# A graph network on one core: layer 3's state and the neighbour sums turned by block transpose and device memory

## The reference, cut to what matters

```python
def first(x, adj, weight, bias):                       # x 16x512x128, adj 16x512x512
    adj_norm = adj / (adj.sum(-1, keepdims=True) + 1e-8)
    h_neigh = einsum('bnm,bmf->bnf', adj_norm, x)
    return relu(concatenate([x, h_neigh], -1) @ weight + bias)

def gated(x, adj, mask, weight, w_ih, w_hh, b_ih, b_hh):
    A = (adj != 0)
    h = x
    for l in range(5):
        m = einsum('bnd,de->bne', h, weight[l])
        agg = einsum('bij,bid->bjd', A, m)
        h = gru_cell(agg, h, w_ih, w_hh, b_ih, b_hh)   # r, z, n gates; (1-z)*n + z*h
    return h * mask[..., None]

x = layernorm(x + first(x, adj, ...))
x = layernorm(x + gated(x, adj, ...))
```

## Time and profile before

| | |
|---|---|
| median of 3 runs | 609.21 us (609.12 to 609.42) |
| the profiled execution | 608.95 us, span 606.9 us |
| PE busy | 589.7 us, 97% of the span |
| DVE busy | 513.5 us, 85% |
| ACT busy | 419.4 us, 69% |
| POOL busy | 419.4 us, 69% |
| chain that ended last | PE 91%, DVE 4%, all else 1% or less each |
| granted TensorE clock | 0.992 of full over the span |

### The profile page before, as it was taken

How to read it: one execution, slowest core, us unless ns; L and a number is a source line. 1 busy time by engine, 2 the same in 40 slices (tenths; PEclk the granted TensorE clock), 3 DMA queues, 4 the chain that set the end, 5 groups by cost and what they waited for, 6 DMA issues and landing times.

```text
span 606.9 us, 9921 instructions
## 1 busy us (share of the span) xinstructions
PE 589.7 (97%) x2733; PEld 479.4 (79%) x2733; DVE 513.5 (85%) x1151; ACT 419.4 (69%) x777; POOL 419.4 (69%) x335
## 2 busy tenths in 40 slices
PE   7999999999999999999999999999999999999992
PEld 6678788888888888888888888888888888877771
DVE  5986969898998989899898989989898898966677
ACT  5767685958778595876868587685867768555451
POOL 0645464878868687886869688687977868755343
PEclk9999999999999999999999999999999999999996
DMA  8713122454344446334444534445453433010101
GB/s 271 294 35 114 54 76 88 134 180 121 123 151 112 161 127 190 121 121 146 115 154 138 190 112 130 141 115 158 138 174 110 148 138 95 10 53 10 44 0 53
DMA packets 74002, 73.55 MB, mean 121 GB/s; under 512 B 5760, under 2 KB 49280, under 8 KB 73984
## 3 DMA queue, kind: packets, MB, share of 16 engines
q1 hardware_dynamic: 73712, 73.20, 37.7%
q10 hardware_dynamic: 272, 0.13, 0.1%
HBM read 56.00 MB, written 17.30 MB: 121 GB/s over the span
## 4 chain that ended last, share of the span: by engine, by line
PE 91%; DVE 4%; DMA 1%; issue 1%; ACT 1%; SPq 1%; POOL 0%; POOLq 0%; DVEq 0%
PE ps_tok L1405 12%; PE ps_tok L1412 12%; PE ps_r L1269 6%; PE ps_r L1270 6%; PE ps_r L1271 6%; PE ps_z L1269 6%; PE ps_z L1271 6%; PE ps_z L1270 6%; PE ps_b L1271 3%; PE ps_b L1269 3%; PE ps_b L1270 3%; PE ps_in L1270 3%; PE ps_in L1271 3%; PE ps_hn L1271 3%; PE ps_in L1269 3%; PE ps_hn L1270 3%
## 5 line engine op out<-in xcount | busy, mean ns | idle before, releaser
L686 POOL TENSOR_TENSOR z_h<-z_gate,h 128x512 f32<-128x512 f32 x80 | 110.2, 1377 | 24.1 <-ACT z_gate L893 24.0
L676 POOL TENSOR_TENSOR h_lo<-h,h_hi 128x512 fp32r<-128x512 f32 x64 | 88.5, 1383 | 53.8 <-ACT h_hi L708 53.8
L811 ACT ACTIVATE ps_in<-ps_in,gru_bias 128x512 f32<-128x512 f32 x80 | 52.8, 660 | 53.6 <-DVE ps_in L1132 53.5
L1405 PE MATMUL ps_tok<-edges,tok_hi 128*128 (+1 forms) x320 | 87.8, 396 | 0.7 <-ACT tok_hi L708 0.7
L1412 PE MATMUL ps_tok<-edges,tok_lo 128*128 (+1 forms) x320 | 87.6, 396 | 0.0
L1248 DVE SCALAR_TENSOR_TENSOR r_hn<-ps_hn,gru_bias,r_gate 128x512 f32<-128x512 f32 x80 | 59.6, 745 | 28.1 <-ACT r_gate L883 26.9
L615 POOL TENSOR_TENSOR adjt_lo<-adjt_in,adjt_hi 128x512 fp32r<-128x512 f32 x56 | 72.1, 1312 | 4.3 <-ACT adjt_hi L708 4.3
L1405 PEld LDWEIGHTS ps_tok<-edges,tok_hi 128*128 128x128 f32 x320 | 59.7, 188 | 15.6 <-ACT tok_hi L708 0.9
L1412 PEld LDWEIGHTS ps_tok<-edges,tok_lo 128*128 128x128 f32 x320 | 59.9, 188 | 14.7 <-DVE tok_lo L919 0.3
L883 ACT ACTIVATE r_gate<-ps_r,rz_bias 128x512 f32<-128x512 f32 x80 | 55.2, 691 | 20.0 <-PE ps_r L1271 17.0
L1173 DVE SCALAR_TENSOR_TENSOR ps_in<-z_gate,ps_in 128x512 f32<-128x512 f32 x80 | 55.1, 689 | 10.9 <-ACT ps_in L811 8.6
(11 more groups left out here) (156 smaller groups left out, 1599.0 us busy)
## 6 DMA issues: line engine op xcount, KB each, us to landing
adjt_in<-in_adj_t_dram SPq DMA_DIRECT2D x14, 1024.0 KB, 5.4
adj_in<-in_adj_dram SPq DMA_DIRECT2D x14, 1024.0 KB, 5.3
rows<-passage SPq DMA_DIRECT2D x144, 64.0 KB, 2.0
passage<-early_blocks SPq DMA_DIRECT2D x24, 256.0 KB, 2.1
x_in<-in_x_dram SPq DMA_DIRECT2D x16, 256.0 KB, 3.8
xt_in<-in_x_t_dram SPq DMA_DIRECT2D x15, 256.0 KB, 3.0
out_dram<-y_out SPq DMA_DIRECT2D x15, 256.0 KB, 2.3
passage<-last_blocks SPq DMA_DIRECT2D x14, 256.0 KB, 2.1
```

Source lines behind the costliest of these rows:

```text
L676: nc.gpsimd.tensor_tensor(h_lo[new][:], h[new][:], raw(h_hi[new][:]), ALU.subtract).then_inc(s_h_lo, 1)
L686: nc.gpsimd.tensor_tensor(z_h[:], z_gate[:], h[own][:], ALU.mult).then_inc(s_zh, 1)
L1405: nc.tensor.matmul(ps_tok[:], tok_hi[:, c * P:(c + 1) * P], edges_from(c, unit[0]), start=c == 0, stop=False)
```

## The change

Slot 4 joins `MOVED`, so that in windows 3 to 14 layer 3's tokens come by block transpose and device memory; DVE turns the blocks in slot 2. In windows 2 to 14 (`means`) the neighbour sums are turned in the same way: DVE turns the blocks of `ps_b[2]` in slot 1, SP stores and loads them into `mean_t`, and `mean_parts` reads them from there, a slot later; ACT's copy of `mean_t` and PE's four matmuls go. The own products stay in PSUM (`own_of`, `residual`, `first_residual`). The edges are made in three pieces (slots 1, 3 and the next slot 0). Sums of the last norm go from slot 1 to slot 2, POOL's `last_norm` from slot 2 to slot 3, behind which `rstd1` now stands after the tokens. SP stores the sums between the store and the load of state 1, and puts state 3 and both loads ahead of the adjacency loads; x is loaded before the adjacency. The scratch of the row sums becomes `r_gate` or `y_out`.

```diff
--- before.py
+++ after.py
@@ -23,7 +23,7 @@
-MOVED = {slot: UNITS[slot][1] for slot in (1, 2, 3)}
+MOVED = {slot: UNITS[slot][1] for slot in (1, 2, 3, 4)}
@@ -143,7 +143,12 @@
             return is_moved(self.batches, self.first + 1, 1)
-        return slot in (0, 1) and self.trips()
+        return slot in (0, 1, 2) and self.trips()
+    def means(self):
+        return self.prepares() and not self.ramps()
@@ -307,8 +312,8 @@
         own = sb("own", [P, C, D])
-        sum_of = sb("sum_of", [P, N])
         mean_t = sb("mean_t", [P, N])
+        mean_rows = mean_t[:].rearrange("p (f c j) -> p f c j", f=4, c=C)
         row_sum = sb("row_sum", [P, C])
@@ -346,9 +351,10 @@
         late_blocks = sb("late_blocks", [P, Q, C, SQ])
-        blocks = {4: early_blocks, 1: early_blocks, 2: late_blocks}
-        passages = {k: nc.dram_tensor(f"passage{k}", [P, N], F32, kind="Internal").ap() for k in (1, 2, 4)}
-        rows = {k: sb(f"rows{k}", [P, Q, C, SQ]) for k in (1, 2, 4)}
+        blocks = {4: early_blocks, 1: early_blocks, 3: early_blocks, 2: late_blocks}
+        mean_passage = nc.dram_tensor("mean_passage", [P, N], F32, kind="Internal").ap()
+        passages = {k: nc.dram_tensor(f"passage{k}", [P, N], F32, kind="Internal").ap() for k in range(1, LAYERS)}
+        rows = {k: sb(f"rows{k}", [P, Q, C, SQ]) for k in range(1, LAYERS)}
...
@@ -430,9 +438,9 @@
         s_last = sem("s_last")
-        s_state_blocks = {k: sem(f"s_state_blocks{k}") for k in (1, 2, 4)}
-        s_state_passed = {k: sem(f"s_state_passed{k}") for k in (1, 2, 4)}
-        s_state_rows = {k: sem(f"s_state_rows{k}") for k in (1, 2, 4)}
+        s_state_blocks = {k: sem(f"s_state_blocks{k}") for k in range(1, LAYERS)}
+        s_state_passed = {k: sem(f"s_state_passed{k}") for k in range(1, LAYERS)}
+        s_state_rows = {k: sem(f"s_state_rows{k}") for k in range(1, LAYERS)}
         s_blocks = sem("s_blocks")
@@ -554,16 +562,24 @@
                     store_state(w, 1)
+                if w.means():
+                    store_blocks(late_blocks, mean_passage, s_nsum_out, w.prepared(1, 1), s_mean_passed)
+                if w.trips():
                     load_state(w, 1)
+                if w.means():
+                    load_rows(mean_rows, mean_passage, s_mean_passed, w.passed(16, 1), s_mean_rows)
+                if w.trips():
+                    store_state(w, 3)
+                    load_state(w, 3)
                 if w.loads():
...
                 if w.loads():
+                    sp.wait_ge(s_pre1, w.prepared(1, 1))
+                    load_x(b)
                     sp.wait_ge(s_row_sum, w.prepared(C, C) if w.first > 0 else C)
...
                     load_adj(b)
-                    sp.wait_ge(s_pre1, w.prepared(1, 1))
-                    load_x(b)
                 if w.finishes():
@@ -661,15 +677,15 @@
                                                     raw(tok_hi[:]), ALU.subtract).then_inc(s_x1_lo, 1)
-                    if w.prepares() and slot == 3 and not w.leads():
-                        rstd1_of_batch()
-                    if w.finishes() and slot == 2 and (w.prepares() or w.idles()):
+                    if w.finishes() and (slot == 3 and w.prepares() or slot == 2 and w.idles()):
                         last_norm()
...
                                                 tokens(raw(tok_hi[:])), ALU.subtract).then_inc(s_tok_lo, 1)
+                    if w.prepares() and slot == 3 and not w.leads():
+                        rstd1_of_batch()
                     if w.unit_before(slot) and made < LAYERS:
@@ -717,7 +733,8 @@
                     act.wait_ge(s_row_sum, earlier)
-                nc.scalar.activation(sum_of[:] if c != 1 or earlier is not None else r_gate[:], of[:, c, :], ACT.Copy,
+                scratch = y_out[:].rearrange("p c d -> p (c d)") if of is second_adj or earlier is None and c == 0 else r_gate[:]
+                nc.scalar.activation(scratch, of[:, c, :], ACT.Copy,
                                      accum_out=row_sum[:, c:c + 1]).then_inc(s_row_sum, 1)
@@ -871,7 +888,7 @@
                         h0_of_batch()
-                    if w.prepares() and slot == 1 and not w.leads():
+                    if slot == 1 and w.first == 1:
                         mean_t_of_batch()
@@ -880,6 +897,8 @@
                             act.wait_ge(s_rhn, w.units(slot))
+                        if slot == 1 and w.prepares() and w.first > 0:
+                            act.wait_ge(s_row_sum, w.prepared(C, C))
                         nc.scalar.activation(r_gate[:], ps_r[:], ACT.Sigmoid, bias=rz_bias[:, 0:1]).then_inc(s_r, 1)
@@ -926,8 +945,9 @@
-            def own_of(half):
-                nc.vector.tensor_tensor(own[:, 2 * half:2 * half + 2, :], parts(half)[:, :, 0, :],
+            def own_of(half, stays=False):
+                nc.vector.tensor_tensor(parts(half)[:, :, 0, :] if stays else own[:, 2 * half:2 * half + 2, :],
+                                        parts(half)[:, :, 0, :],
                                         bias0[:].rearrange("p (o d) -> p o d", o=1).to_broadcast([P, 2, D]),
@@ -986,32 +1006,53 @@
+            def chunk(c):
+                return parts(c // 2)[:, c % 2, 0, :]
             def mean_parts(w):
...
-                dve.wait_ge(s_nsum_tok, w.prepared(1, 1))
                 dve.wait_ge(s_rinv, w.prepared(2, 2))
+                if w.means():
+                    dve.wait_ge(s_mean_rows, w.passed(Q * 16, 1))
+                else:
+                    dve.wait_ge(s_nsum_tok, w.prepared(1, 1))
                 for c in range(C):
-                    last = nc.vector.scalar_tensor_tensor(
-                        out=ps_b[0][:, c * D:(c + 1) * D], in0=ps_b[0][:, c * D:(c + 1) * D],
-                        scalar=row_inv[:, c:c + 1], in1=own[:, c, :], op0=ALU.mult, op1=ALU.add)
+                    if w.means():
+                        mixed = chunk(c).rearrange("p (f j) -> p f j", f=Q)
+                        last = nc.vector.scalar_tensor_tensor(
+                            out=mixed, in0=mean_rows[:, :, c, :],
+                            scalar=row_inv[:, c:c + 1], in1=mixed, op0=ALU.mult, op1=ALU.add)
+                    else:
+                        last = nc.vector.scalar_tensor_tensor(
+                            out=ps_b[0][:, c * D:(c + 1) * D], in0=ps_b[0][:, c * D:(c + 1) * D],
+                            scalar=row_inv[:, c:c + 1], in1=own[:, c, :], op0=ALU.mult, op1=ALU.add)
                 last.then_inc(s_mixed, 1)
...
                 dve.wait_ge(s_mixed, w.prepared(1, 1))
-                nc.vector.scalar_tensor_tensor(out=first_residual(w), in0=ps_b[0][:].rearrange("p (c d) -> p c d", c=C),
-                                               scalar=0.0, in1=x_in[:],
-                                               op0=ALU.max, op1=ALU.add).then_inc(s_pre1, 1)
+                if w.means():
+                    for half in range(2):
+                        mixed = parts(half)[:, :, 0, :]
+                        last = nc.vector.scalar_tensor_tensor(out=mixed, in0=mixed, scalar=0.0,
+                                                              in1=x_in[:, 2 * half:2 * half + 2, :],
+                                                              op0=ALU.max, op1=ALU.add)
+                else:
+                    last = nc.vector.scalar_tensor_tensor(out=pre1[:],
+                                                          in0=ps_b[0][:].rearrange("p (c d) -> p c d", c=C),
+                                                          scalar=0.0, in1=x_in[:], op0=ALU.max, op1=ALU.add)
+                last.then_inc(s_pre1, 1)
                 dve.wait_ge(s_pre1, w.prepared(1, 1))
...
-            def first_residual(w):
-                return pre1[:] if w.ramps() else ps_b[0][:].rearrange("p (c d) -> p c d", c=C)
+            def first_residual(w, c):
+                return chunk(c) if w.means() else pre1[:, c, :]
...
                 for c in cs:
-                    nc.vector.bn_stats(stats1[:, c, :], first_residual(w)[:, c, :]).then_inc(s_stats1, 1)
+                    nc.vector.bn_stats(stats1[:, c, :], first_residual(w, c)).then_inc(s_stats1, 1)
@@ -1024,7 +1065,7 @@
                 for c in range(C):
-                    nc.vector.tensor_scalar(x1[:, c, :], first_residual(w)[:, c, :], mv1[:, c, 0:1],
+                    nc.vector.tensor_scalar(x1[:, c, :], first_residual(w, c), mv1[:, c, 0:1],
                                             rstd1[:, c:c + 1], ALU.subtract, ALU.mult).then_inc(s_x1, 1)
@@ -1037,7 +1078,7 @@
                              y_hi[:, 2 * half:2 * half + 2, 0:D])
-                    own_of(half)
+                    own_of(half, w.means())
@@ -1049,8 +1090,8 @@
                     dve.wait_ge(s_h, w.units(slot))
-                    if slot == 1:
-                        dve.wait_ge(s_state_passed[4], w.passed(16))
+                    if slot in (1, 2):
```

(40 more changed lines are left out.)

## The result

The changed kernel takes 611.25 us (median of 7, 610.17 to 613.24) against 609.21 before: a ratio of 1.0038, 95% interval 1.0023 to 1.0053. It is 2 us slower, where 605.9 and thus a gain was forecast; it lies inside the range. The profiled execution has a span of 608.4 us against 606.9. It is the fastest of the seven (610.17), so what the slower ones lost beyond it is in no trace.

The account below looks back on a forecast made before the run. PE, busy 97% of the span, was taken as the bound. Per window 35.63 - 0.87 + 0.35 + 0.30 = 35.41; 12 x 0.22 + 0.44 = 3.1 us off 608.95 gives 605.9, range 598.0 to 614.5.

Parts of the forecast that it names:

- What PE loses: PE, slots 2 and 3: each set of four turns costs 0.44 us; 25 sets go, 11.0 us, 0.87 per window.
- The chain of slots 3 and 4: DVE, slot 2's `r_hn` to slot 4's `agg_lo`: grows 0.63 to 0.65 against slack 0.30; PE waits 0.35 us per window.
- a wait for `tok_lo`: Sign: the prediction called itself wrong if PE waits for `tok_lo`; it expected PE to wait for `agg_lo` in slot 4.
- DVE's lateness goes round: Rival, slots 0 and 1: edges and norm sums wait for POOL, `r_hn` 0.5 us late; 614.9 us; chance of slower 0.34.
- PE stays the only bound: Rival: everything added on DVE finds cover, so all 11.0 us are gained, 598.0 us; chance 0.14.
- Waits of DVE for POOL: DVE instructions from SBUF to SBUF stand still until POOL's current one ends, 0 to 1.30 us; slot 3's edges taken at 0.30.
- SP's queue: Ten more DMAs per window, 4.2 us to issue; state 1's rows and the adjacency loads come later but stay covered: nothing.

Follow-up runs that it names:

- agg_first: Changed kernel with DVE making `agg_lo` in slot 4 right behind `norm1`, ahead of the product with (z-1): 614.28 us, ratio 1.0092 to the kernel before.
- h0_zh: h0_first with two POOL instructions exchanged (layer 0's low part, `z_h`, other low part): 611.37 us, ratio 1.0041 to the kernel before.
- h0_first: Changed kernel with ACT copying layer 0's state and high part first in slot 4, POOL making layer 0's low part first: 619.64 us, ratio 1.0167 to the kernel before.

## Why the prediction was wrong, point by point

- *What PE loses*: right, 0.44 us for a set of four turns, 25 sets. From window 4 on there is no stall in slots 2 and 3.
- *The chain of slots 3 and 4*: the mechanism was right. Forecast were 0.35 and a wait of 0.30, that is 0.65; slot 4 lost 0.61. That this comes so close is in part luck. In the window shown the chain grew by 0.72, not by 0.93: the edges took 0.62 at 243.93, about 0.2 of it waiting, and the rest came to about 0.5, not 0.63, with 0.15 for the drain ahead of the edges in it. Against that stands a wait that the chain left out. The last norm's variance, moved into slot 2 right in front of `r_hn`, took 0.64 to 1.06 us in windows 3 to 14, where it needs 0.17. In windows 7, 12 and 13 it took over 1 us, and `r_hn` began only 0.03 to 0.08 before slot 3 instead of 0.47; the edges met no wait there (0.43). The timelines of DVE and of POOL in window 7:

```profile
272.79 1.06 DVE L1144 TENSOR_SCALAR var<-mv 128x4 f32<-128x4 f32 x1
273.76 0.74 DVE L1300 SCALAR_TENSOR_TENSOR r_hn<-ps_hn,gru_bias,r_gate 128x512 f32<-128x512 f32 x1
```

```profile
272.52 1.31 POOL L692 TENSOR_TENSOR h_lo<-h,h_hi 128x512 fp32r<-128x512 f32 x1
```

- *The step that failed* is that the chain was ended at `agg_lo`: what hangs behind it in slot 0 stood in the sum at nothing, without a reason. "Slot 4's agg_lo" is followed on DVE by `h`, and behind `h` stand, in ACT's order, its high part, the copy of layer 0, `r_gate` and layer 0's high part, then POOL's low part, then PE's state products of slot 0. Before, that low part was ready 0.48 us (251.62 against 252.10) before PE came to it; the late chain and the shorter slots used this slack up. PE lost 0.34 us in slot 0 of a window, 3.9 us over windows 4 to 15. agg_first shows it as a second deadline (0.79 more in slot 0 once slot 4's stall is gone), h0_zh that an earlier low part takes 0.21 of the 0.34 away.
- *Left out as well*: window 2, which the sum credits with 0.44. Its slot 3 took 7.40 us against 6.46. PE waited 0.8 us for DVE's `tok_lo`, which there still comes from PSUM and now stands behind the norm. The prediction had named a wait for `tok_lo` as a sign of being wrong. Window 3 took 36.14, 0.5 over its neighbours; PE waited there 0.20 and 0.17 us for state 3's token parts, and then for `agg_lo`. The waits of PE in windows 2 and 3:

```profile
PE ps_tok L1457 <- DVE tok_lo L938: 0.8, 1, 0.8
PE ps_r L1321 <- DVE agg_lo L938: 0.2, 1, 0.2
PE ps_tok L1457 <- ACT tok_hi L724: 0.2, 1, 0.2
PE ps_tok L1464 <- POOL tok_lo L685: 0.2, 1, 0.2
```

- The profiled run adds up: against the kernel before, window 2 ends 0.40 late, window 3 adds 0.51, the later ones about 0.05 each, 1.5 in all.
- *The rival "DVE's lateness goes round"* had the sign. It named slot 0, but for the piece of edges there; PE's wait in slot 0 came by way of ACT and POOL. Its late `r_hn` of slot 2 did come, by 0.4 us in three of twelve windows, and behind the variance. *PE stays the only bound* was wrong in every order tried.
- *Waits of DVE for POOL*: right, and more than a term. The Trainium skill ("SBUF — State Buffer", "SBUF: two separate sides") states that of two instructions that contend for the shared port pair the second blocks for the whole of the first; h0_first agrees, 1.84 us for `xt_lo` against 1.00 with POOL's order changed.
- *SP's queue*: the adjacency loads were in time, as forecast (no engine waited for one in windows 3 to 14), but state 3's rows were late once. In window 3 its four loads started as long after the start of slot 3 as in window 6 (0.76 and 0.77 us), took 2.86 us to issue instead of 1.73, and `tok_hi` started 5.71 us into slot 3 instead of 4.07. The first SP row is window 3, the second window 6; the last row is ACT in window 3. Why those loads issued slowly stays open.

```profile
131.12 2.86 SPq L539 DMA_DIRECT2D rows<-passage  x4
...
238.96 1.73 SPq L539 DMA_DIRECT2D rows<-passage  x4
```

```profile
136.07 0.63 ACT L724 ACTIVATE tok_hi<-rows 128x512 fp32r<-128x512 f32 x1 [3.04 <-DMA rows<-passage]
```

## What to carry to other kernels

When an engine with no idle time is relieved, each result it takes from others becomes due earlier. List every deadline in the loop, and follow a late result through all queues to the next place where the bound engine reads what comes of it, past the first wait. Work taken off the critical order (the edges, 0.49 us in slot 4) was worth more than reordering the critical instructions, which only exchanged one deadline for another.

## What the runs showed of the hardware

Some DVE instructions that met a running POOL instruction took up to about one such instruction (1.3 us) longer: `xt_lo`, from two tiles in SBUF, 1.84 us against 0.79; edges of 512 columns, from SBUF to SBUF, 1.57 (at 229.75 in the changed kernel) against 0.41; a variance of four columns 1.02 against 0.17. Others showed no such wait in the changed kernel: the 32x32 block transpose within SBUF (0.71 us each time), the last norm's sums (0.86 to 0.87 for four) and `agg_lo`, which reads PSUM and one tile of SBUF (0.68 to 0.69). The wait isn't a constant that can be added up: when other work moved, POOL's instructions moved too, and the same DVE instruction went from no wait to a whole one.
